# Fourth layer of a six-layer network: the value product turned, the turned keys used as values, and the output projection moved into the batch loop

## The reference

```
c  = ctx @ W_kvc                       # 257 positions x 64, the latent of keys AND values
q' = latent queries folded with W_uk   # so that scores are q' . [c | rope(c @ W_kr)]
p  = softmax over 257 positions of (scores * scale + window mask)
y  = sum over heads of  (p @ c) @ (W_uv @ W_o)
x  = x + y
```

## Time and profile before

| what | value |
|---|---|
| median of three runs | 3135.0 us (3133.33 to 3135.61) |
| the profiled execution | 3138.35 us, its span 3136.5 us |
| mean granted TensorE clock of the execution | 0.863 of full speed |
| busy over the span | PE 2388.4, PEld 1687.6, DVE 2023.6, ACT 1310.9, POOL 590.8 us |
| fourth layer | weights land at about 1514 us, batch loop from about 1573 to 2173 us, second loop to 2248.3 us |

### The profile page before, as it was taken

One profiled execution on the slowest core, in us unless ns is written; L12 is line 12 of the kernel. 1 busy time (PEld: TensorE's weight loads), 2 busy tenths in 40 slices (PEclk: granted clock), 3 DMA queues, 4 the chain that ended last, 5 costly groups with the idle time before them and its releaser, 6 DMA issues.

```text
span 3136.5 us, 53904 instructions
## 1 busy us (share of the span) xinstructions
PE 2388.4 (76%) x16108; PEld 1687.6 (54%) x16108; DVE 2023.6 (65%) x5626; ACT 1310.9 (42%) x3376; POOL 590.8 (19%) x634
## 2 busy tenths in 40 slices
PE   5699999999999782333599999998877536566655
PEld 4666666666666551111377777787755422233322
DVE  3356666666666455666277777773277698777777
ACT  1055555555554443323233334343355534444444
POOL 0011111111110000111022222220044352222222
PEclk9999999999999896667699999997878657767777
DMA  2000000001000001000211111110000130000000
GB/s 79 0 24 23 23 23 23 23 23 23 23 23 9 15 0 50 0 0 0 71 28 31 27 31 27 31 28 11 17 11 10 61 108 1 1 1 1 1 1 27
DMA packets 62257, 71.39 MB, mean 23 GB/s; under 512 B 39802, under 2 KB 41275, under 8 KB 59580
## 3 DMA queue, kind: packets, MB, share of 16 engines
q1 hardware_dynamic: 62140, 70.20, 7.7%
HBM read 63.20 MB, written 2.10 MB: 21 GB/s over the span
## 4 chain that ended last, share of the span: by engine, by line
PE 58%; issue 20%; DVE 15%; ACT 4%; DMA 1%; SPq 1%; DVEq 1%; POOL 1%; POOLq 0%; ACTq 0%
PE ps L613 5%; PE ps L660 5%; PE ps L591 4%; PE ps L600 4%; PE ps L627 4%; PE ps L1534 2%; PE ps L563 2%; PE ps L1588 2%; PE ps L1555 2%; PE ps L1572 2%; PE ps L1589 2%; PE ps L1524 2%; PE ps L1543 2%; PE ps L1967 2%; PE ps L1640 2%
## 5 line engine op out<-in xcount | busy, mean ns | idle before, releaser
L350 ACT ACTIVATE a_pr<-ps,a_nm 128x257 f32<-128x257 f32 x512 | 238.1, 473 | 253.6 <-DVE a_nm L464 253.6
L1325 ACT ACTIVATE d_pr<-d_st,d_nm 128x257 f32<-128x257 f32 x256 | 128.3, 503 | 353.6 <-DVE d_nm L1432 353.6
L473 DVE COPY a_pT<-ps 128x512 f32<-128x512 f32 x256 | 176.3, 689 | 126.5 <-PE ps L627 126.5
L2407 PE MATMUL ps<-f_wt,f_nhT 128*128 128x256 bf16 x512 | 107.3, 350 | 159.3 <-DVE x_all L2307 157.7
L2164 POOL TENSOR_TENSOR f_rg<-f_rg 128x512 f32<-128x512 f32 x128 | 135.4, 1058 | 429.7 <-ACT f_rg L2196 424.9
L613 PE MATMUL ps<-a_kT,a_qbd 32*128 32x289 f32 x1024 | 206.0, 449 | 1.9 <-ACT a_pr L350 0.8
L2398 PE MATMUL ps<-f_wt,f_nxT 128*128 128x512 bf16 x512 | 195.5, 523 | 3.3 <-DVE f_act L2332 2.6
L2407 PEld LDWEIGHTS ps<-f_wt,f_nhT 128*128 128x128 bf16 x512 | 53.2, 117 | 246.7 <-issue 196.0
L464 DVE TENSOR_REDUCE a_nm<-ps 128x2 f32<-128x514 f32 x256 | 174.8, 683 | 0.0
L2202 ACT ACTIVATE f_nhT<-ps 128x512 bf16<-128x512 bf16 x128 | 76.3, 596 | 222.0 <-PE ps L2416 222.0
L660 PE MATMUL ps<-a_pT,a_v 128*32 128x128 f32 x2048 | 161.5, 279 | 0.9 <-DVE a_pT L473 0.9
(11 more groups left out here) (357 smaller groups left out, 6115.4 us busy)
## 6 DMA issues: line engine op xcount, KB each, us to landing
a_cT<-in_ctx SPq DMA_DIRECT2D x64, 257.0 KB, 2.7
d_cT<-in_ctx SPq DMA_DIRECT2D x64, 257.0 KB, 2.6
f_wf<-in_f_w SPq DMA_DIRECT2D x12, 1024.0 KB, 4.8
a_vbd<-a_vself SPq DMA_DIRECT2D x256, 8.0 KB
e_vb<-e_vs SPq DMA_DIRECT2D x256, 8.5 KB
c_wf<-in_c_w SPq DMA_DIRECT2D x3, 1024.0 KB, 7.0
x_all<-in_x SPq DMA_DIRECT2D x1, 2048.0 KB, 8.0
d_wo<-in_d_wo SPq DMA_DIRECT2D x1, 2048.0 KB
```

What stands on the lines that cost most here:

```text
L350: ins = act.activation(pr[j][:, g, :], ps[:, S_BANK[u % 2] + k, S:LK], ACT.Exp, bias=nm[j][:, g:g + 1], accum_out=ssum[j][:, 0, g:g + 1])
L473: dve.tensor_copy(pT[u % 2][:, :, :, :], ps[:, bank, :].rearrange("p (g c q) -> p g c q", g=2, c=2))\
L2407: ins = pe.matmul(ps[:, 7, 0:HID], lhsT=nhT[k2 % 2][:, k, :], rhs=wt[:, 3 * (k2 % NE) + 2, k * HID:k * HID + HID], start=(k == 0), stop=(k ...
```

## The change

1. `values` no longer multiplies the context by the latent weights. The latent part of the finished keys (64 rows of `kc`) is transposed instead: two transposes and one small product with the identity. TensorE waits for `k_half` of b ahead of it (`values_wait`), and the transfer of the next context now waits for `keys` instead of `values`.
2. `weigh` is turned: the values (64 columns) are the stationary operand and the turned probabilities (128 columns) the moving one, so that the result has the latent on the partitions; two groups go side by side into partitions 0 to 63 and 64 to 127.
3. The result can no longer be divided by the sums on VectorE (they would lie along the free axis). So the probabilities are divided before they are turned: VectorE takes the reciprocals half by half, and ScalarE multiplies each group by them (`scale`, four more ACTIVATEs of 128x257 a step). `turn` and `turn_last` wait for that.
4. ScalarE copies the weighed values out (`output_out`, one ACTIVATE a step in place of VectorE's `combine`), already in the layout that the projection needs.
5. `project` stands in the loop: in every fourth step (from the sixth on) TensorE projects the tile that ended two batches ago, between `keys` and `score` half 1; VectorE adds it (`output`) after `scores_out` half 1. Its result lies in the other half of `O_BANK`, so `weigh` half 0 of that step waits until it has been added. The second loop is gone but for the last tile.

```diff
@@ scalar
+            def scale(b, j, u):
+                act.wait_ge(ri_ready.sem, ri_ready.at(b, u + 1))
+                for g in (2 * u, 2 * u + 1):
+                    ins = act.activation(pr[j][:, g, :], pr[j][:, g, :], ACT.Copy, scale=ri[j][:, g:g + 1])
+                ins.then_inc(scaled.sem, 1)
+            def output_out(b, s, tile):
+                act.wait_ge(pv_psum.sem, pv_psum.at(b, 2))
...
+                act.activation(ot[s // BT][:, :, s % BT, :], ps[:, O_BANK, 0:HID].rearrange("p (n q) -> p n q", q=S),
+                               ACT.Copy).then_inc(o_out.sem, 1)
@@ scalar, step
                     ins.then_inc(exp_done.sem, 1)
+                    if u == 0 and not (isinstance(b, int) and b == 0):
+                        scale(b - 1, 1 - j, 1)
+                    if u == 0 and not first:
+                        output_out(b - 2, (s - 2) % 8, tile - (1 if s % BT < 2 else 0))
                     if not (isinstance(b, int) and b == 0):
                         turn_out(b - 1, u, first)
+                scale(b, j, 0)
                 if not (isinstance(b, int) and b == B - 1):
                     distances(b + 1, 1 - j, isinstance(b, int) and b == 0)
@@ vector, step
                 if n > 0:
-                    recip(b - 1, 1 - j)
-                if n > 1:
-                    combine(b - 2, j)
+                    recip(b - 1, 1 - j, 1)
                 values_out(b, j, n < 2)
                 if n < B - 1:
                     keys_out(b + 1, 1 - j, n == 0)
+                recip(b, j, 0)
                 scores_out(b, 1, n == 0)
+                if s % BT == 1 and n > 1:
+                    output(tile - 1)
@@ tensor
+            def values(b, j):
                 for c in range(2):
-                    for k in range(KT):
-                        pe.matmul(ps[:, T_BANK[1], P + c * KVC:P + c * KVC + KVC], lhsT=cT[j][:, k, c * P:c * P + P],
-                                  rhs=kw[:, k, 0:KVC], start=(k == 0), stop=(k == KT - 1))
...
+                    pe.transpose(ps[:, T_BANK[1], P + c * KVC:P + c * KVC + KVC], kc[j][0:KVC, c * P:c * P + P],
+                                 ident[0:KVC, 0:KVC])
@@ tensor, weigh
-                    ins = pe.matmul(dst, lhsT=pT[u][:, k, 1, :], rhs=vc[j][:, 1, :], start=False,
-                                    stop=(g == G1 - 1))
+                for c in range(2):
+                    for k in range(2):
+                        ins = pe.matmul(ps[KVC * k:KVC * k + KVC, O_BANK, u * P:u * P + P], lhsT=vc[j][:, c, :],
+                                        rhs=pT[u][:, k, c, :], start=False, stop=(u == 1 and c == 1),
+                                        skip_group_check=True)
@@ tensor, new
+            def project(t, a, b):
+                pe.wait_ge(o_out.sem, o_out.at(b, 0))
+                for h in range(2 * HA):
+                    ins = pe.matmul(ps[:, O_BANK, Y_AT:Y_AT + HID], lhsT=ot[a][:, h, :, :].rearrange("p b q -> p (b q)"),
+                                    rhs=vo[:, h // HA, h % HA, :], start=(h == 0), stop=(h == 2 * HA - 1))
+                ins.then_inc(y_psum.sem, 1)
@@ tensor, step
                 score(b, j, 0, s, n == 0)
                 if n > 1:
                     weigh(b - 2, j, 1)
-                values(b, j, n == 0)
+                values_wait(b, n == 0)
                 if n > 0:
                     turn(b - 1, 1 - j, 0)
+                values(b, j)
                 if n < B - 1:
                     keys(b + 1, 1 - j, pair)
+                if s % BT == 1 and n > 1:
+                    project(tile - 1, (s - BT) % 8 // BT, b - 1)
                 score(b, j, 1, s, n == 0)
...
                 if n > 0:
                     turn(b - 1, 1 - j, 1)
+                    if s % BT == 1 and n > 1:
+                        layer_wait(pe, 4, tile)
                     weigh(b - 1, 1 - j, 0)
```

More of the change, by code:

```diff
@@ L1187, in latent_attention @@
         pT3 = sb("d_pT3", [G1, P])
[L1188 to L1192, removed]
+        ot = [sb(f"d_ot{j}", [P, 2 * HA, BT, S]) for j in range(2)]
         w_loaded = shared("w_loaded", 16 * 14, 1)
@@ L1335, in scalar @@
             steps(act, step)
+            scale(B - 1, 1, 1)
+            output_out(B - 2, 6, NT - 1)
             for u in range(2):
                 turn_out(B - 1, u)
[L1338 to L1358, removed]
+            output_out(B - 1, 7, NT - 1)
         def vector(dve):
@@ L1408, in last_out, with recip, output @@
                 dve.tensor_copy(pT3[:, :], ps[0:G1, T_BANK[1], 0:P]).then_inc(t3_out.sem, 1)
[L1410 to L1419, removed]
+            def recip(b, j, u):
+                dve.wait_ge(exp_done.sem, exp_done.at(b, u + 1))
+                groups = slice(2 * u, 2 * u + 2)
+                dve.reciprocal(ri[j][:, groups], sm[j][:, groups]).then_inc(ri_ready.sem, 1)
+            def output(t):
+                dve.wait_ge(y_psum.sem, y_psum.at(t, 1))
+                add_to_x(dve, n, t, ps[:, O_BANK, Y_AT:Y_AT + HID])
             def scores_out(b, u, first):
@@ L1465, in vector @@
             steps(dve, step)
-            recip(B - 1, 1)
-            combine(B - 2, 0)
+            recip(B - 1, 1, 1)
             last_out(B - 1)
[L1469 to L1473, removed]
+            output(NT - 1)
         def tensor(pe):
@@ L1559, in turn_last @@
             def turn_last(b, j, values):
+                pe.wait_ge(scaled.sem, scaled.at(b, 2))
                 pe.wait_ge(v_out.sem, v_out.at(values, 1))
@@ L1621, in tensor @@
             weigh(B - 1, 1, 1)
-            def turn_o(t, j, first=False):
-                pe.wait_ge(ot_ready.sem, ot_ready.at(t, 1))
-                if not first:
-                    pe.wait_ge(oT_ready.sem, oT_ready.at(t - 1, 0))
-                for b in range(BT):
-                    for a in range(2):
-                        at = (b % 2) * HID + a * P
-                        ins = pe.transpose(ps[:, TURN_BANK[j] + b // 2, at:at + P], ot[:, j, b, a * P:a * P + P],
-                                           ident[:, :])
-                ins.then_inc(oT_psum.sem, 1)
-            def project(t, j, first=False):
-                pe.wait_ge(oT_ready.sem, oT_ready.at(t, 2))
-                if not first:
-                    layer_wait(pe, n + 1, t - 1)
-                for a in range(2):
-                    for h in range(HA):
-                        ins = pe.matmul(ps[:, Y_BANK[j], 0:HID], lhsT=oT[j][:, a, h, :], rhs=vo[:, a, h, :],
-                                        start=(a == 0 and h == 0), stop=(a == 1 and h == HA - 1))
-                ins.then_inc(y_psum.sem, 1)
-            for j in range(2):
-                turn_o(j, j, first=True)
-            project(0, 0, first=True)
-            with pe.Fori(0, NT // 2 - 1) as i:
-                for j in range(2):
-                    turn_o(i * 2 + (j + 2), j)
-                    project(i * 2 + (j + 1), 1 - j)
-            project(NT - 1, 1)
+            project(NT - 1, 1, B)
         return dict(sp=sp, pool=pool, scalar=scalar, vector=vector, tensor=tensor)
```

30 lines of the change are left out of this document (14 added, 16 removed).

## The result

| | before | after |
|---|---|---|
| median | 3135.31 us (4 runs, 3133.33 to 3136.3) | 3097.86 us (4 runs, 3094.95 to 3107.65) |
| ratio after / before | | 0.9887, 95% interval 0.9864 to 0.9909 |
| profiled execution, its span | 3138.35, 3136.5 us | 3107.65, 3105.8 us |
| batch loop, first score to last `weigh` | 601.1 us (1572.03 to 2173.16) | 637.9 us (1568.44 to 2206.33) |
| last `weigh` to the next layer's first load | 75.2 us | 5.2 us |

Faster by 1.1%, at the forecast time. The tail gave back 70.0 us, the loop took 36.8, so 33.2 are left; the two spans differ by 30.7, the rest lies in other layers. Step lengths in this part are the distances between first scores in the timeline of TensorE. The profiled execution of the kernel after is the longest of its four (3107.65 us; the others took 3094.95 to 3098.93), so its step lengths, taken together, are longer than theirs.

A forecast was written before the change was run, and what follows sets the result against it. TensorE was taken to pace the batch loop. 3138.35 - 64.6 (tail) + 6 (projecting groups) - 5 (first four steps) + 26 (clock) = 3100.8; median 3.35 lower, forecast 3098 us, own range 3080 to 3117, whole range 3048 to 3130.

The forecast's parts named there:

- The tail: Behind the batch loop: 75.2 us shrink to 8.6, giving back 66.6, or 70.1 if the clock is high there.
- `weigh` and `values`: TensorE in a plain step: each `weigh` half 0.56 us instead of 0.84, `values` 0.6 instead of 1.30.
- TensorE paces plain steps at 7.9, the scaling hides with 0.5 to spare: Steps without projection: TensorE needs 7.9 us, ScalarE and VectorE with the scaling 7.4, so the scaling is hidden.
- the 7.4: Plain step's cycle on VectorE and ScalarE, from scores through exponentials, scaling and distances to the mask: 7.4 us.
- TensorE's own 7.9: TensorE's work in a plain step: 0.92 + 0.56 + 0.60 + 0.50 + 2.52 + 2.81 = 7.9 us instead of 9.17.
- The projecting step: 15 of 64 loop steps: TensorE idles 2 us for ScalarE's copy; step 12.8 us, the next 8.5.
- The clock: In the loop, the new gap drops TensorE's clock in three of four projecting steps, 2.3 us each: +26 us.
- The clock holds or the steps tighten: Rival in the loop: no clock loss, 3072 us, or with the copy early enough 3042; chance 0.22 for 3042 to 3080.
- Scaling at 1.2: Rival at ScalarE: scaling takes 1.2 us instead of 0.9, 15 x 0.6 more, 3107; inside the forecast's range, no own chance.
- Changes of tiling mode: Rival on TensorE: four more mode changes cost 0.5 us in 49 plain steps, 24 us, 3122; chance 0.12.
- Slower: Rival in the loop: TensorE loses its clock twice in four steps, 3.2 us each, 70 us more, 3168; chance 0.09.
- no difference: Rival in the loop: the same clock loss with some 2.7 us a group more, about 3135; chance 0.07.

The follow-up runs named there:

- e3: On the changed kernel, GpSimd adds the rotary half to 32 query columns instead of 512, every wait kept; 3081.08 us, 0.9824 of the kernel before.
- e2: On the changed kernel, ScalarE computes the distances ahead of the second scaling instead of behind it; 3068.73 us, 0.9793 of the kernel before.
- e8: On the changed kernel, weighed values copied early, distances ahead of the second scaling, projection behind the second scores; 3030.71 us, 0.9677 of the kernel before.
- e1: On the changed kernel, ScalarE copies the weighed values at its step's start, ahead of the first exponentials; 3066.26 us, 0.9786 of the kernel before.

## Why the prediction was right, and where it was not

**Right in the total (3098 against 3097.9), with errors that cancel, and part of that is luck.** The sum for a profiled execution was 3100.8; the profiled execution took 3107.65. The median came out even so because it lies 9.8 us below that execution and not 3.35 as in the kernel before. By its steps:

- *The tail.* Forecast 75.2 to 8.6, measured to 5.2. The last projection ran at clock 1.00, 3.72 us and not 6.9; the 70.1 given for a high clock is what came.
- *`weigh` and `values`.* 0.56 forecast, 0.58 measured; `values` 0.6 forecast, 0.47 measured. These sizes hold.
- *TensorE paces plain steps at 7.9, the scaling hides with 0.5 to spare.* This step failed. Plain steps take mostly 8.43 to 8.6, mean 8.64 in the repeated part, and ScalarE and VectorE pace them: `turn_last` waits for L1316. The terms of the 7.4 held (tick to tick 3.06; from the second tick 1.10 to the exponentials, 1.00 to `turn_out`, 0.48 to the scaling, 0.80 to the distances, 0.53 to the mask) but "hop and mask 0.4": from the mask's start to the tick it took 1.11 us, and 1.72 one step later. That makes 3.06 + 3.91 + 1.11 = 8.1, and for the later step 3.06 + (1809.17 - 1803.47) = 8.8, where 7.4 stood. e3 and e2 show the cause, and that the cover is there once the mask is ahead of the addition. The prediction had named this as what would make it wrong altogether, the distances last ahead of the mask; here it cost 2 x (8.64 - 8.22) = 0.8 us a group. The stretch does not do it alone: in the last twelve steps, as long as queries are made, the mask still takes 0.79 us behind the addition in plain steps, but the tick follows it by 0.07 us and not by 0.24 to 0.61, and plain steps take 8.00. Why the repeated steps have that time between mask and tick stays open.
- *TensorE's own 7.9.* With the mask free the plain step takes 8.22 and not 7.9. The 0.92 of the score, the 0.50 of the `turn` and the 0.87 of the keys inside the 2.52 were carried over from the kernel before; they came to 1.06, 0.59 and 0.97, 0.33 us more, and `values` came 0.13 below its 0.6 (e8).
- *The projecting step.* Gap 2 us forecast, 1.91 measured, with ScalarE's copy as releaser; 12.8 forecast without the clock, about 13.9 measured; the next step 8.5 against 8.08. Part of the 1.1 is the late mask: e3, which frees the mask and leaves a gap of 0.94 to 1.36 us, has 13.0 to 13.45 but for one step.
- *The clock.* Forecast 26 us: three of four projecting steps at 2.3. Measured: 5 of 15 projections run at 0.50 for a part and cost 1.7 each (15.6 against 13.9), and two next steps take 9.67 and not 8.08, 1.6 each; 11.7 us. Four more drops, which no step of the prediction had, lie in plain steps (from 1652, 1683, 1894 and 1925 us on), behind waits of `turn_last` of 0.84 and 1.1 us; those steps take 8.85 to 9.37, about 3 us in all. The lower clock begins between 0.3 us ahead of the projection's start and 1.0 us behind it, not 2 us behind the gap as was reckoned. Loop clock 0.96 where "near 0.9" stood.
- *The loop's sum.* Over the 12 full groups +41 us measured, +25 forecast (plain and projecting steps dearer, clock cheaper); the rest of the loop -4 against +4. Together +36.8 against +29 with the 2 for its end, and the tail 3.4 better: 4.4 us more than forecast, of the 6.9 by which the profiled execution lies above its sum.

**The rivals.** *The clock holds or the steps tighten*: not as built, but e1 made it so, with two drops of the clock left between 1600 and 2100 us, and came to 3066, above the 3042 worked out for it, since that took plain steps at 7.9. *Scaling at 1.2*: it took 0.90. *Changes of tiling mode*: plain steps are above 8.3 as that rival said, but most of it is idle ahead of `turn_last` that ends with ScalarE; e2 brings steps to 8.2 with all narrow weights in place, and e8's plain steps are no longer. The remaining 0.33 us a step stand where this rival put them, at the changes between full and narrow products, two thirds of the 0.5 it had reckoned. The Trainium skill's rule that changing the tiling mode drains TensorE (TensorEngine Tiling (Array Packing), Key Properties) agrees with that 0.33 us and with the idle of 0.33 us in the weight loads, but no run separates the change of mode from the products' shapes. *Slower* and *no difference*: a group in which both the projecting step and the next one lost time to the clock came twice in 15, not each time.

## What to carry to other kernels

An operation that only becomes later can become longer: look at what another engine does at the new time, and not only at who waits for it. When work moves into a loop, put its operand's copy first and its own place behind the operation that feeds the other engines; here those two moves and one swap were worth 2.1%, twice what the whole change was. And time the parts alone: the values by themselves gave as much as the change with everything.

## What the runs showed of the hardware

- VectorE's mask, a TENSOR_SCALAR of 257 fp32 columns from SBUF to SBUF, takes 0.30 us alone or when it starts first, and, in the kernel after, up to 1.28 when it starts behind GpSimd's TENSOR_TENSOR of 512 columns; it then ends 0.15 us after that one. The one started second takes longer: with the mask first, the addition took 1.37 instead of 1.27. The Trainium skill has this rule, in SBUF — State Buffer, Who interferes with whom: a `tensor_scalar` in its two-port mode and a GpSimd operation take a shared pair of ports as a lock, and the later one blocks. The trace agrees on who waits, with the numbers just given. It does not show the full length of such a block: the mask ends 0.15 us after the addition though it needs 0.30 alone, and the addition takes 0.10 longer where 0.25 of the mask were left; times on GpSimd are rough.
- TensorE's granted clock fell from 1.00 to 0.50 in 5 of the 15 projecting steps, with gaps of 1.91 and 1.92 us ahead of the projection; it did not in one step with 1.92, in four with 1.82 or 1.83, in two with 1.64 and 1.65 and in two with 0.5. What chooses is not shown. With the gap filled no projection ran at 0.50. It also fell behind shorter waits: of 0.84 to 1.12 us in four plain steps of the kernel after, of 1.33 in one projecting step of e3. The gap of 0.5 a step in the kernel before never cost it between 1600 and 2100 us.
- Eight products of 128 columns with 64-column weights, four into each half of the partitions, take 0.58 us, where eight with 64 columns streamed and full weights took 0.84. The full-size scores ahead of them take 0.14 us longer to the next start than they did ahead of full weights.
